# Attention block: transposed inputs read from a host layout instead of being transposed on TensorE

## The chip, the cores and the metric

One core of one Trainium2 chip runs the whole kernel. The metric is the device time of one execution in microseconds, the median of the runs; lower is better. Engines are named as in the profile: PE is TensorE (PEld its weight loads), DVE is VectorE, ACT is ScalarE, POOL is GpSimd, SP is SyncE, which issues every DMA of this kernel.

## The reference, cut to what matters

```python
def _layernorm(x, axis=-1, eps=1e-05):
    m = jnp.mean(x, axis=axis, keepdims=True)
    v = jnp.var(x, axis=axis, keepdims=True)
    return (x - m) / jnp.sqrt(v + eps)
...
        b, n, _ = q.shape
        h, d = (HEADS, DIM_HEAD)
...
        qh = split_heads(q @ Wq)
        kh = split_heads(k @ Wk)
        vh = split_heads(v @ Wv)
        dots = jnp.einsum('bhid,bhjd->bhij', qh, kh) * SCALE
...
        dots = jnp.where(causal[None, None, :, :], mask_value, dots)
        attn = jax.nn.softmax(dots, axis=-1)
        out = jnp.einsum('bhij,bhjd->bhid', attn, vh)
        out = out.transpose(0, 2, 1, 3).reshape(b, n, h * d)
        return out @ Wo + bo
...
    x = x + jnp.tanh(g_xattn[0]) * _L0_xattn_ref(_layernorm(x, axis=-1), ctx_1024, ctx_1024, L0_xattn_Wq, L0_xattn_Wk, L0_xattn_Wv, L0_xattn_Wo, L0_xattn_bo, mask_BxS2_bf0)
    x = x + jnp.tanh(g_ffn[0]) * _L0_ffn_ref(_layernorm(x, axis=-1), L0_ffn_w_gate, L0_ffn_w_up, L0_ffn_w_down)
    return x
```

x and ctx_1024 are (64, 128, 256) in f32, with 16 heads of 64; `_L0_ffn_ref` is a gated feed-forward with quantised weights and activations, which the change does not touch.

The change lies in the first line of the attention: how `layernorm(x)` and `ctx` come into SBUF with the 256 features on partitions, as the products need them.

## The kernel before, in words

The attention takes the 64 batches in G = 16 groups of NB = 4. A group has NC = 8 steps c = 0 to 7, one for each pair of heads, so there are U = 128 steps u = 8g + c. Here "step six" is c = 6 and "step seven" is c = 7, the last of a group. Groups 1 to 14 are a hardware loop with the same instructions each time. The program of each engine is written out by hand (`step` in each engine's block), and engines meet through semaphores alone. It is pipelined over steps: in step u, PE makes the q, k and v products of u and its scores; DVE adds the mask to the scores of u - 1 and takes row maxima (`masked`, `neg_max`), ACT exponentiates (`prob`), DVE inverts the sums (`rsums`), POOL multiplies them in (L386, one instruction for each of two heads); PE transposes the probabilities of u - 2, ACT and DVE copy one head each out of PSUM (`probT`), and PE multiplies with v (`pv`, L813), after which ACT and DVE split the result into a high and a low part (`o_hi`, `o_lo`) for the output product (L840) of the next step. A product in full precision is three passes of high and low parts.

Inputs of the next group are made ready in the last steps of the current one:

- step four and five, DVE: statistics of x (`layernorm_stats`, L531) and the moments (L517 to L525); step five, POOL: `rstd` (L374).
- step six, DVE: `normalise` writes xn in four tensor_scalar instructions (L539).
- step seven, PE: `transpose_in` (L784) turns xn and ctx in four jobs of four 128x128 transposes each into the two banks `proj0` and `proj1`, which the q, k and v products use too; ACT copies each bank as the high part (L420) and DVE subtracts for the low part (L547, `tx_lo` and `tc_lo`), reading PSUM and SBUF.

The residual's input, x plus tanh(g) bo, is `xres`: POOL adds it from `x_in` in step three (L391), after the two multiplications of that step. DVE forms x1 in step two (`residual`, L665), takes its statistics at the end of step three (`second_stats`, L671 and the moments again) and normalises it at the end of step six (`second_norm`, L678, four tensor_scalar instructions), before the masks of step seven. `second_max` (L683) follows at the end of step seven. In group 0, the splitting of the attention weights (`w_low_part`, L508) and the first third of the feed-forward weights' dequantisation stand beside the steps on DVE; group 15 has the rest.

On DVE, xn (L539) stands between the two reciprocals of step six (L582 and L600), and the second norm behind `o_lo` (L606) of the same step, by these lines of `step`:

```python
                if c == 6 and new and more:
                    normalise(g + 1)
...
                if c == YC + 3 and new and not (isinstance(g, int) and g == 0):
                    second_norm(g - 1)
```

## Time and profile before

| what | value |
|---|---|
| runs | 1734.68 us median of 3 (1733.4 to 1737.57) |
| the profiled execution | 1733.58 us; its span 1731.8 us |
| PE busy | 1657.9 us, 96% of the span |
| DVE busy | 1334.1 us, 77% |
| ACT busy | 1162.8 us, 67% |
| POOL busy | 493.5 us, 28% |
| mean granted TensorE clock | 0.982 |
| DMA in the attention | about a tenth of the 16 engines' time |

How to read it: the span is what the profiler saw from the first to the last instruction, and 1.8 us of the execution's time lie around it. The attention takes the first 1150 us or so, the feed-forward stages the rest. A busy share of PE says that some matmul was in flight, and matmuls overlap, so start to start is the better measure of what one costs.

### The profile page before, as it was taken

The page shows a single profiled execution, that of the slowest core. Times are in us where ns is not written, and L with a number is a line of the kernel's source. Part 1 is how long each engine was busy: PE and PEld are TensorE (multiplying, and loading weights), DVE is VectorE, ACT ScalarE, POOL GpSimd, SP SyncE. Part 2 cuts the span into 40 slices and gives each one's busy share as a digit, 9 for nine tenths or more (in the row PEclk, how much of TensorE's full clock was granted, in tenths as well). Part 3 has the DMA queues.
Part 4 walks back from the last instruction along what each step waited for, and adds up shares of the span by engine and source line. Part 5 has one row for each costly group of instructions (what it writes and reads, how often), then busy time and mean ns, then how long its engine had stood idle before and what let it go on. Part 6 is the DMA issues. An engine that isn't in the chain of part 4 may idle for free. (4 is left out here: it accounts for less than half of the span.)

```text
span 1731.8 us, 40384 instructions
## 1 busy us (share of the span) xinstructions
PE 1657.9 (96%) x14196; PEld 1407.6 (81%) x14196; DVE 1334.1 (77%) x2273; ACT 1162.8 (67%) x3061; POOL 493.5 (28%) x367
## 2 busy tenths in 40 slices
PE   8999999999999999999999999989997998986998
PEld 6788888888888888888888888878885876875998
DVE  7867768677777786776867778867887999898785
ACT  5656666666566665666666656657676999895665
POOL 2332323223223233232332322310002765560000
PEclk9999999999999999999999999989998999997999
DMA  4110001001100011010100110026775885664664
GB/s 142 67 40 27 28 22 50 24 26 36 30 34 24 26 36 38 26 36 14 50 24 26 36 38 13 14 86 239 283 276 188 298 289 209 230 248 168 212 212 144
DMA packets 60002, 173.55 MB, mean 100 GB/s; under 512 B 4528, under 2 KB 34352, under 8 KB 57008
## 3 DMA queue, kind: packets, MB, share of 16 engines
q1 hardware_dynamic: 59952, 172.90, 28.9%
q8 instruction: 29, 0.48, 0.1%
q14 instruction: 21, 0.17, 0.0%
HBM read 96.86 MB, written 76.02 MB: 100 GB/s over the span
## 5 line engine op out<-in xcount | busy, mean ns | idle before, releaser
L386 POOL TENSOR_TENSOR prob<-prob,rsums 128x512 f32<-128x512 f32 x254 | 266.7, 1050 | 783.5 <-DVE rsums L582 640.7
L428 ACT ACTIVATE prob<-masked,neg_max 128x128 f32<-128x128 f32 x1024 | 396.4, 391 | 77.5 <-DVE neg_max L560 76.5
L428 ACT ACTIVATION_READ_ACCUMULATOR prob<-masked,neg_max 128x1 f32 x1024 | 194.3, 190 | 0.0
L560 DVE TENSOR_REDUCE neg_max<-masked 128x4 f32<-128x512 f32 x254 | 174.3, 686 | 8.8
L558 DVE TENSOR_TENSOR masked<-score,mask_add 128x512 f32<-128x512 f32 x254 | 172.8, 680 | 0.8
L578 DVE COPY probT<-trans 128x512 f32<-128x512 f32 x126 | 86.9, 690 | 108.7 <-PE trans L792 105.8
L792 PE MATMUL trans<-ident,prob 128*128 128x128 f32 x1024 | 160.3, 279 | 0.9 <-POOL prob L406 0.8
L443 ACT ACTIVATE qT<-proj 128x512 f32<-128x512 f32 x128 | 76.7, 599 | 110.8 <-PE proj L757 110.8
L840 PE MATMUL y<-wo_hi,o_hi 128*128 128x256 f32 x508 | 145.5, 286 | 2.1 <-DVE wo_lo L508 2.0
L813 PEld LDWEIGHTS pv<-probT,v_sb 128*64 128x64 f32 x2048 | 109.7, 136 | 46.4 <-issue 44.3
L813 PE MATMUL pv<-probT,v_sb 128*64 128x128 f32 x2048 | 140.1, 279 | 6.5 <-issue 5.8
L840 PE MATMUL y<-wo_lo,o_hi 128*128 128x256 f32 x508 | 143.1, 282 | 0.0
L840 PE MATMUL y<-wo_hi,o_lo 128*128 128x256 f32 x508 | 142.4, 280 | 0.0
L792 PEld LDWEIGHTS trans<-ident,prob 128*128 128x128 f32 x1024 | 117.2, 140 | 28.7 <-POOL prob L406 1.3
L956 PE MATMUL pair<-xThi,wup_hi 128*128 128x512 f32 x312 | 126.1, 404 | 14.5 <-PEq L1282 5.8
L588 DVE COPY v_sb<-proj 128x512 f32<-128x512 f32 x128 | 88.4, 691 | 61.0 <-PE proj L757 60.7
L437 ACT ACTIVATE probT<-trans 128x512 f32<-128x512 f32 x126 | 75.5, 599 | 84.4 <-PE trans L792 84.4
L466 ACT ACTIVATE o_hi<-pv 128x512 fp32r<-128x512 f32 x126 | 74.8, 593 | 83.9 <-PE pv L813 83.3
L606 DVE TENSOR_TENSOR o_lo<-pv,o_hi 128x512 fp32r<-128x512 f32 x126 | 86.5, 687 | 51.0 <-ACT o_hi L466 50.8
L956 PE MATMUL pair<-xThi,wup_lo 128*128 128x512 f32 x312 | 124.9, 400 | 0.0
L956 PE MATMUL pair<-xTlo,wup_hi 128*128 128x512 f32 x312 | 124.6, 399 | 0.0
L827 PE MATMUL score<-kT,qT 64*64 64x128 f32 (+1 forms) x4096 | 115.3, 250 | 0.0
(251 smaller groups left out, 4588.1 us busy)
## 6 DMA issues: line engine op xcount, KB each, us to landing
gate<-gate_d SPq DMA_DIRECT2D x30, 768.0 KB, 4.5
n_x<-n_x_d SPq DMA_DIRECT2D x25, 512.0 KB, 5.0
gate_d<-stage SPq DMA_DIRECT2D x8, 1536.0 KB, 6.1
n_u_d<-w_raw SPq DMA_DIRECT2D x16, 768.0 KB, 4.0
stage<-n_u_d SPq DMA_DIRECT2D x16, 768.0 KB, 6.3
gate_d<-gate SPq DMA_DIRECT2D x7, 1536.0 KB, 6.1
x_in<-in_x SPq DMA_DIRECT2D x16, 512.0 KB, 3.9
ctx_in<-in_ctx SPq DMA_DIRECT2D x16, 512.0 KB, 3.6
```

The costliest lines, as they stand in the source:

```text
L386: gp.tensor_tensor(pr, pr, rsums[:, h, :].rearrange("p (b o) -> p b o", o=1).broadcast_to([P, NB, P]), ALU.mult).then_inc(normed, 1)
L428: nc.scalar.activation(prob[:, c % 2, h, b, :], masked[:, h, b, :], ACT.Exp, bias=neg_max[:, h, b:b + 1], accum_out=psums[:, h, b:b + 1]). ...
L558: nc.vector.tensor_tensor(masked[:, h], score[h][:], mask_add[:], ALU.add).then_inc(masked_done, 1)
L560: nc.vector.tensor_reduce(neg_max[:, h, :], masked[:, h], X, ALU.max, negate=True).then_inc(max_done, 1)
L578: nc.vector.tensor_copy(probT[:, 1], trans[:]).then_inc(probT_copied[1], 1)
L588: nc.vector.tensor_copy(v_sb[:, n % NB, cols], proj[b][:]).then_inc(copied[b], 1)
L606: nc.vector.tensor_tensor(o_lo[:], hand.banks[1][:], o_hi[:].bitcast(F32), ALU.subtract).then_inc(out_split, 1)
L792: last = nc.tensor.transpose(trans[:, b, :], prob[:, c % 2, h, b, :], ident[:])
L813: last = nc.tensor.matmul(pv[h * HD:(h + 1) * HD, b, :], v_sb[:, b, c * P + h * HD:c * P + (h + 1) * HD], probT[:, h, b, :], start=True, s ...
L827: last = nc.tensor.matmul(score[h][half * HALF:(half + 1) * HALF, b, 0:keys], qT[rows[h], at:at + HALF], kT[rows[h], b * P:b * P + keys], ...
L840: last = nc.tensor.matmul(y[:, e, :], o[s][:, e * P:(e + 1) * P], w[m][:, c * D:(c + 1) * D], start=(c == 0 and j == 0 and e % 2 == 0), st ...
L956: last = nc.tensor.matmul(bank, stat(s, k), mov(m, k), start=(j == 0), stop=(j == len(passes) - 1))
```

## The change

The host gives x and ctx a second time, as columns: (256, 8192) arrays with features outermost. They are loaded with the features on partitions (`xt_in`, `ctx_in`, 128 x 2 x 512), so that only group 0's x is still transposed on PE. The layernorm of x then needs mean and rstd of every row along the free axis, the same on all partitions: they are stored to DRAM (`ln_d`) and loaded again, broadcast to 128 partitions (`ln_rows`, in the handover's first `xin` buffer). POOL subtracts the mean (`centre`) and DVE multiplies with rstd (`normalise`), each in one 128x1024 instruction. The high and low parts are made from SBUF. The statistics and moments of x move to the end of step one, POOL's rstd to step two. `xres` no longer comes from `x_in` but from a third load of x, and POOL's addition moves from step three to step six. SP's loop is written out, and its order of loads and stores is new.

On SP:

```diff
+            def load_xres(g):
+
+                wait_x1(sp, g)
+                sp.dma_start(xres[:], x[bass.ds(g * NB, NB)].rearrange("b p d -> p b d")).then_inc(xres_loaded, 16)
+
+            def spread_moments(g):
+
+                sp.wait_ge(rstd_ready, g + 1)
+                sp.dma_start(ln_d[:, g - 1].rearrange("o e b p -> p (o e) b"), ln[:], allow_slow_non_contiguous=True).then_inc(ln_stored, 16)
+                sp.wait_ge(ln_stored, 16 * g)
+                sp.wait_ge(xn_ready, g)
+                sp.dma_start(hand.xin[:, 0].rearrange("p b d -> p (b d)"),
+                             ln_d[:, g - 1].rearrange("o e b p -> o (e b p)").broadcast_to([P, 2 * T])).then_inc(ln_rows_loaded, 16)
+
             def load_next(g):
...
+                load_rows(g + 1)
+                load_columns(g + 1)
+                store_x1(g - 1)
+                load_xres(g)
+                spread_moments(g + 1)
+                store_xn2(g - 1)
+
+            load_rows(1)
+            load_columns(1)
+            load_xres(0)
+            spread_moments(1)
             sp.wait_ge(w_ready, len(PIECES))
```

On POOL, behind the two multiplications of a step:

```diff
+            def centre(g):
+
+                gp.wait_ge(xt_loaded, 16 * g)
+                gp.wait_ge(ln_rows_loaded, 16 * g)
+                gp.tensor_tensor(xt_in[:], xt_in[:], ln_rows[:, 0:1, :].broadcast_to([P, KC, T]), ALU.subtract).then_inc(x_centred, 1)
...
-                if c == YC and new:
-                    gp.wait_ge(x_loaded, 16 * (g + 1))
-                    wait_x1(gp, g)
-                    gp.tensor_tensor(xres[:], x_in[:], bo_g[:].rearrange("p (o n) -> p o n", o=1).broadcast_to([P, NB, D]),
+                if c == 2 and new and more:
+                    make_rstd(g + 1)
+                if c == 5 and new and more:
+                    centre(g + 1)
+                if c == 6 and new:
+                    gp.wait_ge(xres_loaded, 16 * (g + 1))
+                    gp.tensor_tensor(xres[:], xres[:], bo_g[:].rearrange("p (o n) -> p o n", o=1).broadcast_to([P, NB, D]),
                                      ALU.add).then_inc(xres_ready, 1)
                 if c == YC + 1 and new and not (isinstance(g, int) and g == 0):
                     make_rstd2(g - 1)
-                if c == 5 and new and more:
-                    make_rstd(g + 1)
```

On ACT, in step seven (`ctx_high_part` replaces `high` in the same way, with `ctx_in` as its source):

```diff
+            def x_high_part(g, k):
+
+                if k == 0:
+                    act.wait_ge(xn_ready, g + 1)
+                    b, before = nth(g - 1, last_of("q"))
+                    act.wait_ge(projected[b], before + 1)
+                nc.scalar.activation(t_hi[0][:, k, :], xt_in[:, k, :], ACT.Copy).then_inc(x_high, 1)
...
-                    for i, n in ts[:KC]:
-                        high(g, i, n)
+                    for k in range(KC):
+                        x_high_part(g + 1, k)
```

On DVE:

```diff
+            def normalise(g):
+                dve.wait_ge(x_centred, g)
+                dve.wait_ge(ln_rows_loaded, 16 * g)
+                nc.vector.tensor_tensor(xt_in[:], xt_in[:], ln_rows[:, 1:2, :].broadcast_to([P, KC, T]), ALU.mult).then_inc(xn_ready, 1)
...
+            def x_low_part(g, k):
+                dve.wait_ge(x_high, KC * g + k + 1)
+                nc.vector.tensor_tensor(t_lo[0][:, k, :], xt_in[:, k, :], t_hi[0][:, k, :].bitcast(F32), ALU.subtract).then_inc(x_split, 1)
...
-                if c == 5 and new and more:
-                    layernorm_moments(g + 1)
...
-                if c == 4 and new and more:
+                if c == 1 and new and more:
                     layernorm_stats(g + 1)
+                    layernorm_moments(g + 1)
```

On PE, `transpose_in` and its four calls go, and the first q and k product of a group waits for the new parts itself:

```diff
+                def part_split(k):
+                    if n == 1:
+                        pe.wait_ge(ctx_split, KC * g + k + 1)
+                    elif isinstance(g, int) and g == 0:
+                        pe.wait_ge(copied[k], 1)
+                    else:
+                        pe.wait_ge(x_split, KC * (g - 1) + k + 1)
...
-                if nxt:
-                    transpose_in(g, *ts[0])
...
-                if nxt:
-                    transpose_in(g, *ts[3])
```

Where instructions stand now. POOL in the loop over groups 1 to 14, before; this is from step three to step four (L386 are the multiplications, L391 the addition for `xres`):

```order
L386 TENSOR_TENSOR prob<-prob,rsums 128x512
L389 ISA
L231 REGISTER_ALU
L391 TENSOR_TENSOR xres<-x_in,bo_g 128x1024
L384 ISA
L386 TENSOR_TENSOR prob<-prob,rsums 128x512
```

POOL in the same loop after the change, from the end of step five to step seven (L433 are the multiplications, L425 is `centre`, L441 the addition for `xres`):

```order
L433 TENSOR_TENSOR prob<-prob,rsums 128x512
L423 ISA
L425 TENSOR_TENSOR xt_in<-xt_in,xin 128x1024
L431 ISA
L433 TENSOR_TENSOR prob<-prob,rsums 128x512
L431 REGISTER_ALU
L433 TENSOR_TENSOR prob<-prob,rsums 128x512
L441 TENSOR_TENSOR xres<-xres,bo_g 128x1024
L431 ISA
```

The addition stood behind the second multiplication of step three and stands behind that of step six now; `centre` is new behind that of step five.

DVE in the loop after the change, from the second half of step six into step seven (L672 to L753 are step six: second reciprocal, `o_lo`, `second_norm`; from L634 on the masks of step seven):

```order
L658 RECIPROCAL rsums<-psums 128x4
L612 TENSOR_TENSOR xt_in<-xt_in,xin 128x1024
L672 REGISTER_ALU
L674 RECIPROCAL rsums<-psums 128x4
L680 TENSOR_TENSOR o_lo<-pv,o_hi 128x512
L753 TENSOR_SCALAR xn2<-x1,mean2,rstd2 128x256 x4
L632 ISA
L50 ISA
L634 TENSOR_TENSOR masked<-score0,mask_add 128x512
L636 TENSOR_REDUCE neg_max<-masked 128x4
L619 ISA
L620 TENSOR_TENSOR tx_lo<-xt_in,tx_hi 128x512
```

Before, `L539 TENSOR_SCALAR xn<-x_in,mean,rstd 128x256 x4` stood where L612 stands, and `tx_lo` read a PSUM bank; the places are the same.

## Rows read from the trace of the kernel before

**Rows 1.** Stretch: length, busy PE, PEld, DVE, ACT, POOL, then PEclk, DMA share, GB/s.

```profile
505.00:575.00 70.00, 69.51 (x705) 58.73 (x704) 51.98 (x112) 45.32 (x164) 21.04 (x19) 1.00 0.09 31
```

**Rows 2.** Timeline of PE, steps six and seven of group 6; start, duration, idle before.

```profile
486.90 0.66 PE L792 MATMUL trans<-ident,prob 128*128 128x128 f32 x4
...
493.95 0.66 PE L792 MATMUL trans<-ident,prob 128*128 128x128 f32 x4
...
499.52 0.60 PE L792 MATMUL trans<-ident,prob 128*128 128x128 f32 x4
...
501.00 0.66 PE L784 MATMUL proj<-ident,ctx_in 128*128 128x128 f32 x4 [0.45 <-ACT kT L456]
501.59 1.09 PE L813 MATMUL pv<-probT,v_sb 128*64 128x128 f32 x16
...
503.51 0.63 PE L792 MATMUL trans<-ident,prob 128*128 128x128 f32 x4
```

**Rows 3.** Timeline of DVE in the same two steps.

```profile
491.47 2.08 DVE L539 TENSOR_SCALAR xn<-x_in,mean,rstd 128x256 f32<-128x256 f32 x4
...
494.48 1.40 DVE L678 TENSOR_SCALAR xn<-x,mean,rstd 128x256 f32<-128x256 f32 x4
495.80 0.68 DVE L558 TENSOR_TENSOR masked<-score,mask_add 128x512 f32<-128x512 f32 x1
...
499.16 0.68 DVE L547 TENSOR_TENSOR tx_lo<-proj,tx_hi 128x512 fp32r<-128x512 f32 x1
500.15 0.69 DVE L578 COPY probT<-trans 128x512 f32<-128x512 f32 x1 [0.32 <-PE trans L792]
```

**Rows 4.** Timeline of POOL: step six of group 6, and step three of group 7.

```profile
491.63 1.12 POOL L386 TENSOR_TENSOR prob<-prob,rsums 128x512 f32<-128x512 f32 x1 [2.75 <-DVE rsums L582]
493.71 1.04 POOL L386 TENSOR_TENSOR prob<-prob,rsums 128x512 f32<-128x512 f32 x1 [0.96 <-DVE rsums L600]
...
540.15 2.39 POOL L391 TENSOR_TENSOR xres<-x_in,bo_g 128x1024 f32<-128x1024 f32 x1
```

**Rows 5.** All instructions of lines L539 and L678: duration min/median/max in ns.

```profile
L539 DVE TENSOR_SCALAR xn<-x_in,mean,rstd x64: 382/402/1132, 7.9 to 1054.5; 128x256 f32<-128x256 f32 x64
L678 DVE TENSOR_SCALAR xn<-x,mean,rstd x64: 398/401/445, 143.7 to 1154.5; 128x256 f32<-128x256 f32 x64
```

**Rows 6.** Timeline of DVE: step two, and the moments behind step three, of group 7.

```profile
528.46 0.69 DVE L578 COPY probT<-trans 128x512 f32<-128x512 f32 x1 [2.08 <-PE trans L792]
...
542.00 0.57 DVE L517 TENSOR_TENSOR m_sum<-stats 128x4 f32<-128x4 f32 x1
542.49 0.15 DVE L518 TENSOR_TENSOR m_dif<-stats 128x4 f32<-128x4 f32 x1
```

**Rows 7.** Timeline of DVE and POOL in group 0, step one.

```profile
28.48 1.23 DVE L508 TENSOR_TENSOR wv_lo<-v_sb,wv_hi 128x1024 fp32r<-128x1024 f32 x1
28.56 2.04 POOL L386 TENSOR_TENSOR prob<-prob,rsums 128x512 f32<-128x512 f32 x1 [1.68 <-DVE rsums L600]
```

**Rows 8.** Timeline of PE behind three idle times; the last matmul is at half clock.

```profile
39.54 0.39 PE L840 MATMUL y<-wo_hi,o_hi 128*128 128x256 f32 x1 [2.02 <-DVE wo_lo L508]
...
64.10 1.09 PE L813 MATMUL pv<-probT,v_sb 128*64 128x128 f32 x16 [2.75 <-issue]
...
1519.49 0.50 PE L956 MATMUL pair<-xThi,wup_hi 128*128 128x512 f32 x1 [2.15 <-POOL xTlo L1709]
...
1521.00 0.63 PE L956 MATMUL pair<-xThi,wup_lo 128*128 128x512 f32 x1
```

**Rows 9.** Busy time and granted clock behind the idle time at 1517 us.

```profile
1519.90:1523.30 3.40, 3.40 (x10) 2.63 (x9) 3.23 (x4) 3.40 (x5) 3.40 (x2) 0.50 0.92 293
```

**Rows 10.** Timeline of PE: the first q product of group 0.

```profile
13.81 0.47 PE L757 MATMUL proj<-tx_hi,wq_hi 128*128 128x512 f32 x1 [0.97 <-DVE tc_lo L547]
```

**Rows 11.** DMA issues: count, KB each, median us to landing.

```profile
x_in<-in_x SPq DMA_DIRECT2D x16, 512.0 KB, 3.9
...
tg<-in_g_ffn SPq DMA_DIRECT2D x1, 0.5 KB, 7.5
```

More of the change, by code:

```diff
@@ L71, in __init__, with attention @@
         self.x_transposed = sem("x_transposed")
-def attention(nc, x, ctx, mask, g_xattn, wq, wk, wv, wo, bo, w_ffn, ident, ones, x1_d, xn2_d, w_raw, amax_x, wd, hand):
+def attention(nc, x, x_t, ctx_t, mask, g_xattn, wq, wk, wv, wo, bo, w_ffn, ident, ones, x1_d, xn2_d, w_raw, ln_d, amax_x, wd, hand):
     B, S, D = x.shape
@@ L91, in attention @@
     for c in range(NC):
-        jobs += [(c, "q", 0)]
-        if c == NC - 1:
-            jobs += [(c, "t", n) for n in range(KC)]
-        jobs += [(c, "k", 0)]
+        jobs += [(c, "q", 0), (c, "k", 0)]
         if c < 2:
@@ L99, in attention @@
             jobs += [(c, "v", NB + c - 2)]
-    jobs += [(NC - 1, "t", n) for n in range(KC, 2 * KC)]
     NJ = len(jobs)
-    FIRST = 2 * KC
-    last_k = jobs.index((NC - 1, "k", 0))
-    assert NJ % 2 == 0 and FIRST % 2 == 0
-    def first_job(n):
-        return NJ - FIRST + n
+    FIRST = KC
+    assert NJ % 2 == 0 and FIRST == 2
     def jobs_of(c, kind):
@@ L130, in attention @@
         x_in = sb("x_in", [P, NB, D])
-        ctx_in = sb("ctx_in", [P, NB, D])
-        xn = sb("xn", [P, NB, D])
+        ctx_in = sb("ctx_in", [P, KC, T])
+        xt_in = sb("xt_in", [P, KC, T])
+        ln_rows = hand.xin[:, 0].rearrange("p b d -> p (b d)").rearrange("p (e t) -> p e t", e=2)
+        ln = sb("ln", [P, 2, NB])
+        mean, rstd = (ln[:, n, :] for n in range(2))
         xres = sb("xres", [P, NB, D])
@@ L340, in _ @@
                              w.rearrange("(c p) n -> p c n", p=P)).then_inc(ffn_loaded, 16)
-            load_next(0)
-            with sp.Fori(1, G - 1) as i:
+            for i in range(1, G - 1):
                 load_next(i)
-                store(i - 1)
-            store(G - 2)
+            store_x1(G - 2)
+            load_xres(G - 1)
+            store_xn2(G - 2)
             for b in range(2):
@@ L471, in _ @@
             w_high_part(1)
-            for n in range(2 * KC):
-                high(-1, first_job(n), n)
+            for k in range(KC):
+                x_high_first(k)
+            for k in range(KC):
+                ctx_high_part(0, k)
             w_high_part(2)
@@ L510, in _, with moments @@
             MOMENTS = NB + 6
-            def moments(stats, mean, var_eps, done, n, ready):
+            def moments(stats, mean, var_eps, done, n, ready, read=None):
                 v = nc.vector
@@ L520, in moments @@
                 dve.wait_ge(done, n + 3)
-                v.tensor_scalar(mean[:], m_sum[:], 0.5, None, ALU.mult).then_inc(done, 1)
+                if read is not None:
+                    wait(dve, *read)
+                v.tensor_scalar(mean, m_sum[:], 0.5, None, ALU.mult).then_inc(done, 1)
                 v.tensor_tensor(m_sq[:], m_dif[:], m_dif[:], ALU.mult).then_inc(done, 1)
@@ L690, in _ @@
             w_low_part(0)
-            normalise(0)
+            normalise_first()
             w_low_part(1)
-            for n in range(2 * KC):
-                low(-1, first_job(n), n, n)
+            for k in range(KC):
+                x_low_first(k)
+            for k in range(KC):
+                ctx_low_part(0, k)
             w_low_part(2)
@@ L846, in step @@
                 co = (c - 2) % NC
-                nxt = c == NC - 1 and new and more
-                ts = jobs_of(c, "t")
                 first = isinstance(g, int) and g == 0 and c == 0
@@ L2044, in program @@
         w_raw = sb("w_raw", [P, 3 * IC * D])
+        peak = [st.enter_context(nc.semaphore(f"amax_{n}")) for n in ("local", "row", "top", "all")]
         before_n_p = ExitStack()
         hand = Handover(nc, before_n_p, G, D, KC, IC)
-        attention(nc, x, ctx, mask, g_xattn, wq, wk, wv, wo, bo, (w_up, w_gate, w_down), ident, ones, x1_d, xn2_d, w_raw, amax_x, wd, hand)
+        attention(nc, x, x_t, ctx_t, mask, g_xattn, wq, wk, wv, wo, bo, (w_up, w_gate, w_down), ident, ones, x1_d, xn2_d, w_raw, ln_d, amax_x, wd, hand)
         gate = sb("gate", [P, N])
@@ L2113 @@
     inputs["x"] = halves_swapped(np, np.asarray(inputs["x"]))
+    for name, of in (("x_columns", "x"), ("ctx_columns", "ctx_1024")):
+        a = np.asarray(inputs[of])
+        inputs[name] = a.transpose(2, 0, 1).reshape(a.shape[2], -1)
     for name in INPUTS:
```

176 lines of the change are left out of this document (93 added, 83 removed).

## The prediction

> **What bounds the kernel now.** I read the page's table of engines and its slices first: PE is busy for 96% of the span, and in the attention nearly always. The busy times by stretch then show that one group of 70.2 us has PE at work for 69.51 of 70 us at full clock, DVE for 51.98, POOL for 21.04, and the DMA engines for a tenth [rows 1]. So in the attention the time is PE's list of matmuls, as long as every other engine delivers in time. The third view is PE's timeline over the last two steps of a group. Step six goes from 486.90 to 493.95, 7.05 us; step seven, with the same products, goes from 493.95 to 503.51, 9.56 us [rows 2]. The difference of 2.51 us is the sixteen transposes, the slower matmul behind each job, and a wait of 0.45 us for a bank. It comes 15 times (groups 0 to 14): 37.7 us is what the change can win at most in the steady part. The last view is the timeline of DVE and POOL beside these two steps [rows 3, 4], since it decides how much of it is kept.
>
> **What PE can keep.** Without the transposes, the probabilities' second transposition of step seven would start 0.88 us earlier, at 498.64 (two jobs of four transposes before it, 0.36 us each, and 0.08 us for the matmul behind each), end at 499.24, and pv could start about then. But pv needs DVE's copy of probT. DVE works without a gap from 494.48: second_norm, two masks with their maxima, tx_lo twice; only behind the last of these, from 499.16, is the copy's turn, at 499.76, since an instruction of this size lets the next one in after 0.6 us [rows 3]. The change leaves this chain as it is: the same instructions in the same order, and tx_lo(0) comes behind masks that end when it starts anyway. The copy takes 0.69 us and pv starts 0.1 us later: masks at 495.80 mean pv at 500.55, that is 4.75 us after the first mask. Before, pv started at 501.59 [rows 2]. So even undisturbed the gain is 1.04 us a group and not 2.51.
>
> **What POOL does to DVE.** In step six, DVE's four tensor_scalars for xn took 2.08 us, while the four for the second norm, of the same form, took 1.40 [rows 3]. One instruction of xn takes 1.13 us where the median is 0.40, and none of the second norm takes more than 0.445 [rows 5]. The long one falls under POOL's multiplication from 491.63 to 492.75: DVE's first was under way, POOL came next, and DVE's second was held until POOL had finished [rows 4]. The moments show the same: m_sum, a tensor_tensor of 4 columns, takes 0.57 us behind POOL's addition of 540.15 to 542.54, its neighbour 0.15 [rows 4, 6]. The reverse is in group 0: POOL's multiplication takes 2.04 us instead of 1.04 while DVE's subtraction of 128x1024 holds it off [rows 7]. So whichever starts first makes the other wait for its whole instruction.
>
> Now the addition for xres, 2.39 us [rows 4], stands behind POOL's second multiplication of step six, and DVE's second norm is in the same place. Step by step: normalise, one 128x1024 instruction of 1.23 us as in [rows 7], starts at 491.47 and holds POOL's first multiplication until 492.6; the two multiplications end at about 493.6 and 494.65; the addition runs from there to 497.05. DVE starts its first tensor_scalar at 494.48, gets it through, and stands until 497.05 with the other three, which take 0.33 us each: the masks of step seven start at 498.05 instead of 495.80, 2.25 us late. DVE has no gap in which to win that back. pv starts at 498.05 + 4.75 = 502.8, and the step ends 1.92 us later, as before (501.59 to 503.51), at 504.7. Step seven is **1.2 us longer than before**, not 2.5 shorter. What comes next is in time: ACT's high parts of ctx and o_hi shift with pv, and o_lo is wanted only behind the next q product, 1.9 us into step zero. tc_lo, with two operands in SBUF now, can hold POOL's multiplication to about 504.4, just ahead of its use at 504.7.
>
> The Trainium skill, page "SBUF — State Buffer", section "Who interferes with whom", says that DVE and GpSimd share one pair of ports, that whoever issues first has it for the whole instruction, and that a DVE instruction with two SBUF inputs contends with a GpSimd one that reads SBUF. By that rule the new low parts and normalise contend where the old low parts, reading PSUM, did not; the trace agrees on m_sum. The same section of the Trainium skill has a tensor_scalar contend only in a two-port mode; by that the second norm would not be held, and the sum would be the first rival's.
>
> **The other parts.**
> - Statistics and moments, some 2.3 us, move behind step one. DVE has 2.08 us of idle time ahead of probT in step two [rows 6]; the copy would start 0.2 to 0.3 us later and still end before pv (529.4 against 529.75). Cost 0. The same work leaves steps four and five, and with xres gone from step three m_sum is not held there for 0.4 us, which lets pv of step four, now 0.1 us late, start on time: minus 0.1 us a group.
> - rstd moves to step two and centre (2.4 us) to the end of step five: POOL is idle for 2.75 us ahead of step six's multiplications [rows 4]. There DVE reads PSUM for the masks, and the maxima have one input. Cost 0; if the cover went, POOL's first multiplication of step six would be late by what centre overruns.
> - The moments' way over DRAM: rstd is ready in step two, near 534, and centre wants the rows at the end of step five, near 557. The load of 512 KB takes about 3.9 us; the store moves 1024 elements of 4 bytes. The one row with such elements has 128 of them landing in 7.5 us [rows 11]. Ends: 3.9 us, if it is a small transfer like others, and eight times 7.5 = 60 us. I take 8 us, by the nearest row, with the load 12 of the 23 us. SP stands in its queue meanwhile; behind it is only the store of xn2, wanted in step six.
> - More DMA: x twice more and 512 KB of rows a group on engines that are used to a tenth [rows 1]. Cost 0.
> - Four semaphore waits of PE inside the first products of a group: long satisfied. 0, at most 0.1 us each.
> - Start: PE need not transpose ctx and does not wait 0.97 us for tc_lo [rows 10]: 1.2 to 2.2 us earlier. Against that, the statistics of group 1 come ahead of the masks of step two and of wo_lo, for which PE waits already [rows 8], so about 2 us are lost again, and the feed-forward weights are loaded up to 6 us later. Between -2 and +3 us; I take -0.5.
> - Group 0 has another instruction than the second norm there, which gets in ahead of POOL, but then tx_lo waits: +0.3. Group 15 has the same hold and no new inputs: between 0 and 2.25, I take 1.6.
>
> **The clock.** With the hold, PE stands in step seven from 499.24 to 502.8, 3.55 us. An idle time of 2.15 us at 1517 is followed by 3.4 us at a granted clock of 0.50, the 1.2 GHz level, with matmuls of 0.63 us [rows 8, 9]; idle times of 2.02 and 2.75 us in the attention are followed by none [rows 8]. So the clock can fall behind 3.5 us, not always. One fall costs some 1.6 us: half of 3.4 us, a little less where its begin lies in the idle time. Per group the ends are 0 and 1.6; I take two falls in three, 10 of 15.
>
> **The sum.** 14 groups x (1.2 - 0.1) = 15.4; group 0 +0.3; group 15 +1.6; start -0.5: together 16.8. Falls of the clock: 10 x 1.6 = 16. On the profiled 1733.6 us that is 1766.4, and the median of the runs stands 1.1 above that execution: **1767.5 us**.
>
> **The rivals.**
> 1. **No hold (faster).** A tensor_scalar that is not in a two-port mode is not held by POOL. Its pace, 0.33 us for 256 elements, is hardly better than the masks' 0.6 us for 512, which speaks for one element a cycle and against a two-port mode, and then it would not contend. Then masks stay at 495.80, each of 15 groups wins 1.04 + 0.1, group 15 nothing, the start 0.5: 17.6 us, 1717. It turns on whether the hold is under 1.0 us. Against it: an instruction of just this form took 1.13 us in each group, under POOL's. Chance 0.17.
> 2. **Hold, but the clock stays up.** The same without falls: 1734.7 + 16.8 = 1751.5. For it: the idle time of 2.75 us without a fall. Chance 0.22.
> 3. **The hold shorter**, so that it about cancels the 1.04 us (POOL's addition starts late, or DVE gets two instructions in): within 5 us of before, 1735. Chance 0.08.
> 4. **The moments come late.** If the store takes over 19 us, POOL waits in step five with the next multiplications behind it; each us beyond costs 15. At 22 us, 1767 + 45 = 1812. Speaks against it: only 4 KB. Chance 0.05.
>
> **How the numbers follow.** My forecast has 0.48. A measurement of this kernel can tell about 0.3%, 5 us, from no change. Slower: 0.48 + 0.22 + 0.05 = 0.75, faster 0.17, the same 0.08. The range reaches from 1730, which takes in rivals 2 and 3, to 1790, which is a fall in every group (8 us more) with a few long ones, and the upper ends of the start and of the waits; left out are the faster case and the late moments. The forecast's own range is 1756 to 1785.
>
> **What would show it.** In the profile after: no L784-like transposes in step seven; second_norm's four instructions taking some 3.6 us instead of 1.40, with one of them over 2 us, and POOL's xres beside it; pv in step seven with an idle time of PE of about 3.5 us; a group of about 71.3 us where the clock holds and near 73 where it falls; stretches of 0.5 in the clock before 1150 us. I am wrong if second_norm still takes 1.40 us (then rival 1, a group of 69.05 us), if the clock is 1.00 throughout (rival 2), or if PE waits at step five or six for POOL's multiplication (rival 4).

## The result and the profile after

| | before | changed |
|---|---|---|
| runs | 1734.48 us median (1733.4 to 1737.57) | 1785.35 us median of 4 (1784.47 to 1788.7) |
| ratio to before | | 1.0294, 95% interval 1.0275 to 1.0313 |
| profiled execution; its span | 1733.58; 1731.8 us | 1784.8; 1783.0 us |
| mean granted TensorE clock | 0.982 | 0.963 |

The change costs 2.9%, or 50.9 us. The first lines of the changed kernel's page:

```profile
span 1783.0 us, 39738 instructions
...
PE 1662.0 (93%) x13948; PEld 1406.2 (79%) x13948; DVE 1356.1 (76%) x2228; ACT 1163.6 (65%) x3061; POOL 546.2 (31%) x382
...
PEclk9999999999999999999999999998998999898999
```

PE is busy for 4.1 us more than before although it has 13948 matmuls instead of 14196, and stands idle for 47 us more. Where this comes in, the mask `mask_add` shows best: it is computed once in each group, in step zero, by two instructions. Its row in the kernel before, and in the changed one (the two numbers behind the durations are the first and the last start, in group 1 and group 15):

```profile
L570 DVE SCALAR_TENSOR_TENSOR mask_add<-mask_u,causal x30: 414/416/419, 86.6 to 1070.1; 128x256 f32<-128x256 uint8 x30
```

```profile
L646 DVE SCALAR_TENSOR_TENSOR mask_add<-mask_u,causal x30: 415/418/422, 95.1 to 1120.2; 128x256 f32<-128x256 uint8 x30
```

Of the 51.2 us by which the span grew, 8.5 are there when group 1 begins, 41.6 come in groups 1 to 14 (1025.1 us instead of 983.5: **73.22 us a group instead of 70.25**), and 1.1 behind them.

Inside a group, steps six and seven on DVE and POOL of the changed kernel, against [rows 3, 4]:

```profile
519.63 0.18 DVE L674 RECIPROCAL rsums<-psums 128x4 f32<-128x4 f32 x1 [0.54 <-ACT prob L491]
520.27 0.69 DVE L680 TENSOR_TENSOR o_lo<-pv,o_hi 128x512 fp32r<-128x512 f32 x1 [0.47 <-ACT o_hi L528]
520.88 3.57 DVE L753 TENSOR_SCALAR xn<-x,mean,rstd 128x256 f32<-128x256 f32 x4
524.37 0.68 DVE L634 TENSOR_TENSOR masked<-score,mask_add 128x512 f32<-128x512 f32 x1
...
528.21 0.68 DVE L654 COPY probT<-trans 128x512 f32<-128x512 f32 x1
```

```profile
518.05 2.93 POOL L433 TENSOR_TENSOR prob<-prob,rsums 128x512 f32<-128x512 f32 x2 [2.28 <-DVE rsums L658]
520.94 2.39 POOL L441 TENSOR_TENSOR xres<-xres,bo_g 128x1024 f32<-128x1024 f32 x1
```

DVE's first tensor_scalar of the second norm starts at 520.88, POOL's addition for xres at 520.94, and the next tensor_scalar runs when POOL is done, near 523.3. The last of the three numbers in the next row is the longest, 2600 ns, where the median is 402; one of the four instructions took about that in each of groups 1 to 14 (14 of the 64):

```profile
L753 DVE TENSOR_SCALAR xn<-x,mean,rstd x64: 399/402/2600, 153.2 to 1207.7; 128x256 f32<-128x256 f32 x64
```

What PE makes of it, in the same group (`pv` of steps six, seven and zero), and its waits for pv from 80 to 1160 us (total, times, longest):

```profile
518.50 1.09 PE L897 MATMUL pv<-probT,v_sb 128*64 128x128 f32 x16
528.99 1.98 PE L897 MATMUL pv<-probT,v_sb 128*64 128x128 f32 x16 [3.31 <-issue]
540.38 1.09 PE L897 MATMUL pv<-probT,v_sb 128*64 128x128 f32 x16
```

```profile
PE pv L897 <- issue: 48.7, 15, 3.3
```

From pv to pv, step seven takes 10.49 us; before, 9.49 [rows 2]. The wait of 3.31 us comes 14 times. Behind it, in this group, the sixteen matmuls of pv take 1.98 us instead of 1.09: the clock has fallen. Busy times by stretch show it in two lengths (behind PE, the times of PEld, DVE, ACT and POOL; then the granted clock, the DMA engines' share and GB/s):

```profile
160.20:167.00 6.80, 5.68 (x56) 4.96 (x57) 5.95 (x10) 3.83 (x13) 2.39 (x2) 0.50 0.12 42
235.30:238.70 3.40, 3.38 (x48) 2.95 (x48) 2.59 (x4) 2.13 (x8) 2.40 (x2) 0.50 0.00 0
```

0.50 is the 1.2 GHz level. There are twelve such stretches in groups 1 to 14, six of 6.8 us and six of 3.4. In the kernel before there is none from the start to 1158 us. Two of the 14 groups have none here either; the time at which one of them would stand:

```profile
820.00:830.00 10.00, 9.67 (x92) 8.20 (x92) 8.84 (x16) 7.11 (x29) 2.95 (x3) 1.00 0.02 5
```

And the beginning. SP's queue in the kernel before, then SP, DVE and PE of the changed one:

```profile
39.51 0.38 SPq L339 DMA_DIRECT2D w_raw<-in_L_ffn_w_up  x1
```

```profile
41.01 0.37 SPq L359 DMA_DIRECT2D ln_d<-ln  x1
49.86 0.33 SPq L362 DMA_DIRECT2D xin<-ln_d  x1
50.23 0.43 SPq L379 DMA_DIRECT2D w_raw<-in_L_ffn_w_up  x1
```

```profile
64.32 1.75 DVE L707 TENSOR_REDUCE w_max<-w_raw 128x48 f32<-128x1536 f32 x1 [3.65 <-DMA w_raw<-in_L_ffn_w_down]
```

```profile
17.01 0.76 PE L836 MATMUL proj<-wv_hi,tc_hi 128*128 128x512 f32 x1 [2.35 <-DVE wq_lo L572]
...
37.01 1.09 PE L897 MATMUL pv<-probT,v_sb 128*64 128x128 f32 x16 [1.57 <-DVE probT L654]
43.32 0.39 PE L924 MATMUL y<-wo_hi,o_hi 128*128 128x256 f32 x1 [2.40 <-DVE wo_lo L572]
71.92 1.97 PE L897 MATMUL pv<-probT,v_sb 128*64 128x128 f32 x16 [5.14 <-issue]
```

SP waits 8.85 us for the store of the moments to end, and the feed-forward weights stand behind it; DVE waits for them for 3.65 us, and PE in step five of group 0 for 5.14 instead of 2.75 [rows 8]. Three of PE's waits, of 2.35, 2.40 and 5.14 us, have a fall of the clock beside them, which the kernel before has nowhere in group 0:

```profile
16.80:20.20 3.40, 3.19 (x8) 2.55 (x9) 1.14 (x4) 2.13 (x3) 1.14 (x1) 0.50 0.57 168
44.10:47.50 3.40, 3.40 (x13) 2.95 (x12) 1.77 (x3) 1.65 (x8) 0.00 (x0) 0.50 0.00 0
71.40:74.80 3.40, 2.88 (x42) 2.58 (x46) 1.50 (x5) 2.85 (x12) 1.90 (x2) 0.51 0.02 5
```

### The profile page after: what moved, and what is told of

Read it like the earlier page. It is cut to its first block and busy times, and to the rows that moved or that the text cites. A ratio compares the mean times of both kernels' runs of the same rounds, so it can differ in the third digit from the quotient of the medians.

```text
span 1783.0 us, 39738 instructions
## 1 busy us (share of the span) xinstructions
PE 1662.0 (93%) x13948; PEld 1406.2 (79%) x13948; DVE 1356.1 (76%) x2228; ACT 1163.6 (65%) x3061; POOL 546.2 (31%) x382
## 2 busy tenths in 40 slices
DMA packets 86195, 197.74 MB, mean 111 GB/s; under 512 B 20864, under 2 KB 50688, under 8 KB 83200
## 5 line engine op out<-in xcount | busy, mean ns | idle before, releaser
L433 POOL TENSOR_TENSOR prob<-prob,rsums 128x512 f32<-128x512 f32 x254 | 283.1, 1119 | 783.6 <-DVE rsums L658 680.2
L897 PE MATMUL pv<-probT,v_sb 128*64 128x128 f32 x2048 | 151.9, 294 | 59.1 <-issue 57.6
L897 PEld LDWEIGHTS pv<-probT,v_sb 128*64 128x64 f32 x2048 | 119.3, 145 | 99.7 <-issue 97.6
L634 DVE TENSOR_TENSOR masked<-score,mask_add 128x512 f32<-128x512 f32 x254 | 173.2, 682 | 1.6
L876 PE MATMUL trans<-ident,prob 128*128 128x128 f32 x1024 | 164.0, 284 | 0.8 <-ACT probT L547 0.8
L528 ACT ACTIVATE o_hi<-pv 128x512 fp32r<-128x512 f32 x126 | 74.6, 592 | 91.2 <-PE pv L897 90.3
L911 PE MATMUL score<-kT,qT 64*64 64x128 f32 (+1 forms) x4096 | 124.2, 263 | 0.0
```

Source lines behind the costliest of these rows:

```text
L433: gp.tensor_tensor(pr, pr, rsums[:, h, :].rearrange("p (b o) -> p b o", o=1).broadcast_to([P, NB, P]), ALU.mult).then_inc(normed, 1)
L634: nc.vector.tensor_tensor(masked[:, h], score[h][:], mask_add[:], ALU.add).then_inc(masked_done, 1)
L876: last = nc.tensor.transpose(trans[:, b, :], prob[:, c % 2, h, b, :], ident[:])
L897: last = nc.tensor.matmul(pv[h * HD:(h + 1) * HD, b, :], v_sb[:, b, c * P + h * HD:c * P + (h + 1) * HD], probT[:, h, b, :], start=True, s ...
L911: last = nc.tensor.matmul(score[h][half * HALF:(half + 1) * HALF, b, 0:keys], qT[rows[h], at:at + HALF], kT[rows[h], b * P:b * P + keys], ...
```

## The experiments

Theory A, the prediction's: POOL's addition holds DVE's second norm, DVE's chain up to the copy of probT makes pv late, and PE's idle time brings the clock down. The rivals: the addition costs by its place on POOL and not by what it meets; the group is longer for some other reason (DMA, semaphores); the falls are all of it.

### The addition in step four

```diff
-                if c == 6 and new:
+                if c == 4 and new:
```

> The changed kernel with one move undone in kind: POOL's addition for xres stands behind the multiplications of step four, where DVE has no instruction that it can hold, and not in step six. If the hold of the second norm is the cause (and the clock falls are its consequence): second_norm takes 1.40 us for its four again, pv of step seven starts about 1.0 us earlier than in the kernel before, a group of the loop takes 69.1 us instead of 73.2, no fall of the clock in groups 1 to 14, and the time is about 1724 us (14 x 4.1 = 57 less than 1785, and some 3 us more from the ends). If the loss lies in the low parts read from SBUF, in the way of the moments over DRAM or in the moved statistics: second_norm shorter but the group stays near 73 us and the time above 1770.

Measured: 1730.82 us (1727.89 to 1735.58), ratio to the kernel before 0.9983 (0.9972 to 0.9993). One line takes 54 us off. A group is 69.62 us and the clock stays up in all of the loop. The second norm of this kernel, and pv of step seven:

```profile
499.95 1.38 DVE L753 TENSOR_SCALAR xn<-x,mean,rstd 128x256 f32<-128x256 f32 x4
```

```profile
497.57 1.09 PE L897 MATMUL pv<-probT,v_sb 128*64 128x128 f32 x16
506.08 1.09 PE L897 MATMUL pv<-probT,v_sb 128*64 128x128 f32 x16 [1.33 <-issue]
516.10 1.09 PE L897 MATMUL pv<-probT,v_sb 128*64 128x128 f32 x16
```

Step seven is now 0.98 us shorter than before (8.51 against 9.49), the 1.04 us that the prediction had for the undisturbed case. The time missed its expectation by 7 us all the same, since the group won only 0.63: against the kernel before, step zero is longer by 0.19 us and the steps one to six by 0.17 together (medians of groups 2 to 14). The start, 95.3 us to the first mask, still has its 8.7 us.

### The addition in step three, its old place

```diff
-                if c == 6 and new:
+                if c == 3 and new:
```

> The same addition in step three, where the kernel before had it. The hold theory has it within 2 us of the kernel with the addition in step four, slower by 0.1 us a group (1.5 us), because m_sum of the moments behind step three is held for 0.4 us again and the step after it starts pv 0.1 us late: about 1725.5 us. If DVE's slack there were smaller than the trace of before shows, it would be up to 6 us slower than the other.

Measured: 1735.74 us (1731.61 to 1739.58), ratio 1.0011 (0.9999 to 1.0023), a group of 70.04 us, step seven again 8.50. That is 5 us more than with the addition in step four, and the profile puts it into the groups (0.42 us each) and the start (1.5 us, first mask at 96.8). The difference does not lie in every group: the median group takes 69.57 us here and 69.54 with the addition in step four. It lies in a few, from 70.8 to 71.4 us long. In two of these the addition comes before its operand, the third load of x, has landed, and PE's pv of step four then waits 1.76 and 1.84 us; one of the two:

```profile
691.03 2.40 POOL L441 TENSOR_TENSOR xres<-xres,bo_g 128x1024 f32<-128x1024 f32 x1 [1.79 <-DMA xres<-in_x]
```

So in step three DVE's slack is enough and the load is what is late, in some groups. In the third long group ACT waits (last section).

### The hold put into the kernel before

```diff
+                if c == 6 and not isinstance(g, int):
+                    row = bo_g[:].rearrange("p (o n) -> p o n", o=1).broadcast_to([P, NB, D])
+                    gp.tensor_tensor(hand.xin[:, 1], row, row, ALU.add)
```

> The kernel before, with one POOL instruction more in step six of groups 1 to 14, behind the two multiplications: an addition of 128x1024 (2.4 us) from and to SBUF, whose result nobody reads. No other part of the change. If POOL's instruction alone holds the second norm: second_norm's four take 3.6 us, the masks of step seven come 2.25 us late, pv of step seven 1.2 us late; a group takes 71.4 us instead of 70.2, the time is about 1751 us, with few falls of the clock since the transposes of ctx break up PE's idle time. If the hold needs the change's other parts, or a fourth instruction of POOL is hidden as in step three: 1735 us.

Measured: 1745.94 us (1741.82 to 1746.97), ratio 1.0073 (1.0054 to 1.0093). The three lines of POOL, DVE and PE:

```profile
499.34 1.94 POOL L397 TENSOR_TENSOR xin<-bo_g 128x1024 f32<-128x1024 f32 x1
```

```profile
499.09 2.99 DVE L681 TENSOR_SCALAR xn<-x,mean,rstd 128x256 f32<-128x256 f32 x4
```

```profile
504.05 0.50 PE L760 MATMUL proj<-tc_hi,wk_hi 128*128 128x512 f32 x1 [1.15 <-DVE tx_lo L550]
```

So the hold alone, without host layout, moments or new DMAs, makes the kernel before slower: 0.86 us a group, and 11.9 us in all against the 1734.02 us of the kernel before, measured beside it. The addition was 0.45 us shorter here than xres's (1.94 against 2.39), and the group lost about that much less than 1.2. PE's idle time of 1.15 us brought no fall.

### PE kept busy through the wait

32 transposes of the identity into a free bank, ahead of pv in step seven of the changed kernel; the hold stays.

```diff
+                if c == NC - 1 and new and more:
...
+                    for n in range(FILL):
+                        nc.tensor.transpose(proj[b][:, (n % NB) * P:(n % NB + 1) * P], ident[:], ident[:])
```

> The changed kernel as it is, with 32 transposes of the identity (2.9 us) put into the idle time of PE in step seven, into the bank of the q product after ACT has copied it; they compute nothing that is used. It keeps the hold and takes the idle time away from the clock. Theory: second_norm still 3.6 us, pv of step seven where it was or 0.1 us later, but granted clock 1.00 in groups 1 to 14; a group takes 71.4 us (70.2 + 1.2) instead of 73.2 and the time is about 1759 us. If the slow stretches cost nothing because PE has slack behind them: 1785 as before. If the hold costs more than I think and the clock less: between 1765 and 1785.

Measured: 1763.34 us (1761.86 to 1764.44), ratio 1.0169 (1.0149 to 1.0189).

```profile
517.37 3.66 PE L965 MATMUL proj<-ident 128*128 128x128 f32 x32
520.95 1.09 PE L898 MATMUL pv<-probT,v_sb 128*64 128x128 f32 x16
...
530.90 1.09 PE L898 MATMUL pv<-probT,v_sb 128*64 128x128 f32 x16
```

With work that computes nothing, the kernel is 22 us faster: no fall in the loop, a group of 71.78 us. Step seven is 10.60 us, 0.11 longer for the transposes. Step zero is 9.95 us; with a fall of 3.4 us it took 11.39 (528.99 to 540.38 above), with one of 6.8 us 12.40. So **one fall costs 1.44 or 2.45 us**, by its length, and six of each are 23.3 us; the loop shows 20.2, and the transposes' 0.11 us account for half of the difference.

### Place or meeting: the second norm moved away

In the changed kernel the addition stays in step six; the second norm goes to step five, behind the copy of v.

```diff
+                if c == YC + 2 and new and not (isinstance(g, int) and g == 0):
+                    second_norm(g - 1)
...
-                if c == YC + 3 and new and not (isinstance(g, int) and g == 0):
-                    second_norm(g - 1)
```

> The changed kernel with the second norm in step five, and POOL's addition for xres left in step six. It tells whether the addition costs by its place or by what it meets. If only what meets it is held (the tensor_scalars had one SBUF source), the addition now stands beside the masks of step seven, which read PSUM, and the first tx_lo, with two SBUF sources, which it holds for up to 1.5 us: pv of step seven late by 0 to 1.3 us, a group between 68.3 and 69.8 us, 1712 to 1733 us; no fall of the clock in groups 1 to 14. If the addition costs wherever it lies in step six (POOL late for the next multiplications, or masks held as well), step seven stays above 10 us and the time above 1760 us.

Measured: 1735.5 us (1731.05 to 1739.06), ratio 1.0002 (0.999 to 1.0013), a group of 69.78 us, no fall.

```profile
504.29 2.40 POOL L441 TENSOR_TENSOR xres<-xres,bo_g 128x1024 f32<-128x1024 f32 x1
```

```profile
504.22 0.68 DVE L634 TENSOR_TENSOR masked<-score,mask_add 128x512 f32<-128x512 f32 x1
504.94 0.69 DVE L636 TENSOR_REDUCE neg_max<-masked 128x4 f32<-128x512 f32 x1
507.04 0.69 DVE L620 TENSOR_TENSOR tx_lo<-xt_in,tx_hi 128x512 fp32r<-128x512 f32 x1 [1.41 <-ACT tx_hi L474]
```

The addition lies where it lay, as long as ever, and costs nothing: the mask reads PSUM, the maximum has one source, and both keep their 0.68 us. It was the meeting.

### Both moves, and the next bound

> The changed kernel with POOL's addition for xres in step four (as before) and with the second norm's four tensor_scalars moved from the end of step six to step five, ahead of the reciprocal. With the addition alone in step four, pv of step seven still came 1.33 us after PE was ready for it, behind the chain second norm, masks, tx_lo, copy of probT. Theory of the chain: without the second norm's 1.4 us in it the masks start 1.3 us earlier and that wait goes: step seven (pv of step six to pv of step seven) 7.2 us instead of 8.51, a group of 68.3 us, 1730.8 - 14 x 1.3 = 1712 us. Rival: DVE passes the lateness on (masks of step six 0.6 us later, then ACT and POOL late in step six), and at most half of it is won: 1721 us or more.

Measured: 1732.98 us (1729.63 to 1737.13), ratio 0.9989 (0.9977 to 1.0). The theory of the chain fell in this form: step seven is 8.50 us, as with the norm in its place. The last row above shows why, and it is the same in this kernel: DVE is free 1.4 us earlier and spends just that waiting for ACT's tx_hi, which waits for PE's q product of the step. Two bounds lay on one another. The next two edits take them in turn. They stand on the kernel with both moves and with the weights loaded first (next section), which takes 1725.2 us:

```diff
-                        if nxt:
-                            x_low_part(g + 1, h)
+                    if nxt:
+                        for k in range(KC):
+                            x_low_part(g + 1, k)
```

> All three edits (POOL's addition for xres in step four, second norm in step five, SP's loads of the feed-forward weights first) and a fourth: in step seven DVE makes both parts of tx_lo behind the second mask and its maximum, no longer one part behind each mask. What I had missed, read from the trace without this edit: with the second norm gone DVE stands idle for 1.41 us in step seven, in the wait of the first tx_lo for ACT's tx_hi, which itself waits behind qT for PE; the second mask, tx_lo and the copy of probT queue behind it, and pv still comes 1.32 us late. Theory: with the masks ahead, DVE is free when tx_hi comes, both tx_lo end before the transposition does (503.7 in that trace), the copy starts at once and pv at 504.4 instead of 504.99: 0.6 us a group, 15 times, 1725.2 - 9 = 1716 us, a group of 69.15 us. Rival: the copy of probT is then released by PE itself, and what is left (0.7 us or more) is latency; nothing more is won if tx_lo delays the copy or POOL's multiplications: 1722 us or more.

Measured: 1726.84 us (1724.13 to 1730.03), ratio 0.9955 (0.9937 to 0.9972), against 0.9949 without this edit (next section). pv comes 0.5 us earlier in step seven, and PE waits in step zero instead:

```profile
500.85 1.09 PE L898 MATMUL pv<-probT,v_sb 128*64 128x128 f32 x16 [0.83 <-issue]
```

```profile
503.15 1.32 DVE L624 TENSOR_TENSOR tc_lo<-ctx_in,tc_hi 128x512 fp32r<-128x512 f32 x1 [0.34 <-ACT tc_hi L483]
504.40 0.68 DVE L683 TENSOR_TENSOR o_lo<-pv,o_hi 128x512 fp32r<-128x512 f32 x1
```

```profile
505.13 0.39 PE L925 MATMUL y<-wo_hi,o_hi 128*128 128x256 f32 x1 [0.33 <-DVE o_lo L683]
```

tc_lo, with two SBUF sources, is held by POOL's multiplication (1.32 us; 0.68 alone), and o_lo stands behind it. So o_lo was put ahead of the second tc_lo:

```diff
-                if nxt:
-                    ctx_low_part(g + 1, 1)
                 if old:
...
+                if nxt:
+                    ctx_low_part(g + 1, 1)
```

> The kernel with the four edits, and a fifth: DVE makes o_lo ahead of the second part of tc_lo. In the kernel with four, pv of step seven came 0.5 us earlier, as expected (8.01 us after the pv before it, not 8.50), but the next step took 10.55 us instead of 10.03: the second tc_lo, with two SBUF sources, is held by POOL's multiplication (1.32 us instead of 0.68), o_lo comes behind it at 3.55 us after pv, and PE's output products wait for o_lo. Theory: o_lo now starts when ACT's o_hi is there, 2.8 us after pv, the wait goes and with it the 0.5 us: step zero 10.03 us, a group of 69.2 us, 1726.8 - 7.5 = 1719 us. Rival: the wait moves on (tc_lo late for the k product, or o_hi behind ACT's second tc_hi), and the group stays within 0.15 us of 69.69: 1725 us or more.

Measured: 1725.83 us (1723.03 to 1726.44), ratio 0.9938 (0.9924 to 0.9951). o_lo is in time, and step zero still takes 10.33 us: now ACT waits 1.9 us for DVE's row maxima, kT is late, and PE waits for it. The rival held: 0.07 us a group on average. The median group did win 0.22 us (69.57 to 69.35), and two long groups of this execution, of 70.3 and 70.6 us, took most of it back. A reading of these runs, and no more, is that DVE, ACT and PE bound the end of a group within half a microsecond of each other.

### The weights loaded ahead of the moments

On the kernel with both moves:

```diff
             load_xres(0)
-            spread_moments(1)
             sp.wait_ge(w_ready, len(PIECES))
             for n, w in enumerate(w_ffn):
...
+            spread_moments(1)
             for i in range(1, G - 1):
```

> The kernel just named, with one more edit on SP's queue: the store and load of group 1's moments stand behind the loads of the feed-forward weights, not ahead of them. Theory: the round trip of the store (8.85 us in the trace of the changed kernel) held those loads up, and with them DVE's maxima of the weights in group 0, and pv of that group (5.1 us idle, followed by a fall of the clock). Then the first group is shorter by 2.5 to 5 us: 1708 us. Rival: the weights were wanted late anyway, and what group 0 lost comes from the statistics of group 1 ahead of the masks of step two: no difference beyond 1 us.

Measured: 1725.2 us (1724.49 to 1729.39), ratio 0.9949 (0.9933 to 0.9965): 7.8 us less than without. The first mask of group 1 stands at 88.7 us instead of 94.0, which is 5.3 of them. That is more than the scatter: the six kernels with the moments and their store of single elements first have it between 94.0 and 97.9 us, the four with the weights first between 88.7 and 91.2. The fall at 71 us is gone in all four. DVE's maxima of the weights start at 59.09 without a wait:

```profile
59.09 1.74 DVE L707 TENSOR_REDUCE w_max<-w_raw 128x48 f32<-128x1536 f32 x1
```

### The store of single elements

```diff
-                sp.dma_start(ln_d[:, g - 1].rearrange("o e b p -> p (o e) b"), ln[:], allow_slow_non_contiguous=True).then_inc(ln_stored, 16)
+                sp.dma_start(ln_d[:, g - 1].rearrange("o e b (q r) -> (o e b q) r", r=8), ln[:].rearrange("p e b -> p (e b)")).then_inc(ln_stored, 16)
```

> The changed kernel with one line altered: the store of the moments to DRAM writes each partition's eight numbers as one run of 32 bytes, 128 runs in all, and no longer 1024 single elements of 4 bytes. This leaves out their order: the rows that come back are mixed, and the layernorm of x is computed with wrong moments; every instruction but the store keeps its size. Theory: the store of single elements takes 9 to 10 us to its end, holds back the loads of the feed-forward weights in group 0, and under it ACT waits 2.5 to 4.3 us for something outside the engines in 5 of the 14 loop groups, each time until about the store's end. With runs of 32 bytes the store ends in 2 to 3 us, the loads go out 6 us earlier, ACT's waits are gone: start 3 to 6 us shorter, the groups 0.1 us: 1785.4 - 6 = 1779 us, still slower than before by over 2%, since the hold and the falls of the clock stay. Rival: the 9 us are latency of two transfers and a semaphore, whatever the size of a run; then nothing changes, 1785 us, and ACT's waits remain.

Measured: 1782.63 us (1782.28 to 1783.96), ratio 1.027 (1.0253 to 1.0287). The store of the changed kernel and this one's, each with the load behind it, in the same group:

```profile
559.81 0.34 SPq L359 DMA_DIRECT2D ln_d<-ln  x1
562.68 0.34 SPq L362 DMA_DIRECT2D xin<-ln_d  x1
```

Like the next one, this kernel leaves out the order of the moments, so that its result is not the layernorm. The store ends within 2.9 us, where the changed kernel's takes 10.2 (563.11 to 573.31), and the first mask of group 1 stands at 90.7 instead of 95.1, 4.4 us earlier, as expected. The groups did not follow: with all of them nearly alike, the clock now falls in all 14 (seven times 6.8, seven times 3.4 us), and a group takes 73.55 us.

> The same store in the kernel with the five edits (1725.8 us), again with the moments' order left out. There the weights are loaded first, so that the start can win little; ACT's waits (2.6 to 5.2 us in 6 of 14 loop groups) cost PE up to 1.2 us each where its slack of two or three us is used up. Theory: they go with the single elements: 1 to 4 us less, 1723 us, group 69.4 us instead of 69.64. Rival: no change beyond 1 us.

Measured: 1723.47 us (1721.35 to 1726.59), ratio 0.9926 (0.9909 to 0.9942), a group of 69.42 us instead of 69.64. ACT's waits are gone in both kernels. The time and the group are as expected, though the gain of 0.12 points in the ratio lies within the two intervals.

## Why the prediction was right, and where its sizes were off

- **The hold.** Right in mechanism, place and size: the second norm takes 3.57 us, 3.6 foreseen; the long one 2.60, over 2 foreseen; pv's idle time 3.31, 3.55 foreseen; step seven 1.00 us longer, 1.2 foreseen. The removed addition, the one put into the kernel before and the moved norm show it from three sides. The prediction set it against the page "SBUF — State Buffer" of the Trainium skill, section "Who interferes with whom", by which a DVE instruction with one SBUF input does not contend outside the two-port modes. The same section of the Trainium skill names tensor_scalar among the instructions that can enter such a mode, so it does not say that the second norm would go free; that conclusion rested on the pace alone. No row here says in which mode it ran, but held it was, and rival 1 was wrong. On tc_lo and POOL's multiplication the same section agrees with the trace (1.32 against 0.68 us).
- **What the group wins beside it** (−0.1 us a group). Too good. Without hold and falls a group wins 0.63 us where the prediction's steps give 1.14: step four won 0.06 (0.1 foreseen), step zero lost 0.19, and the other steps lost 0.03 to 0.07 each, which the prediction had at nothing. It is not the new semaphore waits: they stand in the first products of a group alone. PE's products themselves start farther apart. With the addition in step four, the q or k product with a low part of x or ctx starts 231 to 235 ns after the product before it, in every step; in the kernel before it was 226 to 229. Over all products this is about 0.3 us a group, an estimate from the mean distances in the two traces. Why they do, no run shows. In step zero the held tc_lo also makes o_lo late, by 0.1 us for PE. In the changed kernel this is 0.4 us a group, 6 us of the 51.
- **The clock** (10 falls of 1.6 us = 16). Right in kind, too small in size: 12 falls in the loop, and 14 once the groups are nearly alike. A short one costs 1.44 us, near the 1.6 foreseen; half of them are twice as long and cost 2.45, which the prediction knew only as the range's upper edge. Shown by the filled wait: 20 to 22 us. Three more falls stand in group 0, where the prediction had none.
- **The start** (−0.5, range −2 to +3). Wrong, and outside its own range: +8.5 us. The step that failed is "the feed-forward weights are loaded up to 6 us later", which was costed at nothing of its own: they were 10.7 us later (50.23 against 39.51), behind the store's 8.85 us on SP's queue. The reordered queue gives 5.3 us back, the wide store 4.4. A second step failed before it. PE's lead came as foreseen, with the first q product at 11.63 us instead of 13.81, but it was gone at the first v product (17.01, before 16.80), which waited for DVE's split of the weights. The first pv then came 3.4 us late (37.01, before 33.61) and the second 5.3 (49.7, before 44.4), with two of the three falls on the way. These losses (wq_lo 2.35 us, wo_lo 2.40, probT at 37.01) are in the trace, but no run took them away.
- **The moments over DRAM** (8 us for the store). 8.9 in group 0 and 10.2 in group 7. In time for centre, so rival 4 was wrong; the guess from one row was good, and the same 8 us were not carried to the start, where something was queued behind them.
- **Costs set to nothing**: statistics and moments in step two, m_sum (at most 168 ns now), centre in step five, and the DMA engines' load cost nothing in the loop that these traces show. The third load of x is late in single groups, and that costs where the addition stands early (step three).

The sum was 1767.5 and the measurement 1785.35: just outside the forecast's own range of 1756 to 1785, and inside the wide one, whose upper end was set for a fall in every group and a late start. A rise of 33 us was forecast and 51 came. Of the difference, 9 us are the start, some 7 the other steps of the groups, 4 to 7 the falls; the hold itself was 3 too high.

## What to carry to other kernels

Before placing an instruction on POOL, look at what DVE runs beside it, not only at whether POOL has a gap: 2.4 us of POOL's work cost 54 us beside the second norm, and nothing in another step or beside work on PSUM. An idle time of PE has to be priced with what the clock does behind it, and filling it can pay even when the end of the wait stays. And a move that takes one item off a tight chain wins only the distance to the next bound, so price that one before counting the gain.

## What the hardware showed beyond that

**ACT waits under a store of single elements.** In the changed kernel and in its variants with this store, ACT stands still in some groups until something that is no engine ("remote"). In the kernel with both moves, three of them, and on SP's queue the store of the second one's group and the load behind it, issued when the store had ended:

```profile
199.69 0.60 ACT L500 ACTIVATE probT<-trans 128x512 f32<-128x512 f32 x1 [3.75 <-remote]
548.87 0.60 ACT L500 ACTIVATE probT<-trans 128x512 f32<-128x512 f32 x1 [5.20 <-remote]
757.59 0.60 ACT L500 ACTIVATE probT<-trans 128x512 f32<-128x512 f32 x1 [3.75 <-remote]
```

```profile
537.74 0.37 SPq L359 DMA_DIRECT2D ln_d<-ln  x1
548.91 0.34 SPq L362 DMA_DIRECT2D xin<-ln_d  x1
```

All eight such waits in groups 1 to 14 of that kernel, in seven groups, end within 2 us of the store's end. The kernel before has none, and with runs of 32 bytes (72755 packets instead of 86195) there is none either. They made groups uneven: with the store of 32-byte runs all 14 groups of the changed kernel have a fall. The waits came in five groups and the clock stayed up in two, so how the one brings the other isn't shown. What ACT waits for stays open. That it is ACT's instructions, loaded by DMA, is a guess, and the trace speaks against it: between 170 and 1060 us, where seven of the eight waits lie, the queues of kind "instruction" moved a single packet.

**Fewer and longer runs end sooner.** In the changed kernel 1024 elements of 4 bytes took 8.9 to 12 us to the store's end. The same 4 KB as 128 runs of 32 bytes took 1.4 us in group 0, 4.0 in group 1 and 2.7 to 3.2 in the others. Number and size changed together, so these runs don't tell which of them it is. The Trainium skill, page "DMA: Bandwidth & Descriptors", names 512 bytes as the least for full rate; both stores are far below it, and still differ by some 7 us.

**The clock's falls come in two lengths.** The same idle time of 3.31 us was followed by 3.4 and by 6.8 us at 1.2 GHz in turn, and in two of 14 groups by none; an idle time of 1.33 or 1.15 us in every group was followed by none. Between them the length alone doesn't tell: in group 0 of the changed kernel idle times of 2.35 and 2.40 us have a fall beside them, while 2.02 and 2.75 us had none in the kernel before [rows 8].
